# Hybrid attention and feed-forward kernel: when the feed-forward stage prepares what the window attention needs

## The chip, the cores and the metric

The kernel runs on one core of a Trainium2 chip, as one launch. The metric is the device time of the whole program in microseconds (us). Beside it stands the profile of one execution. The engines are called by their names: TensorE (PE), VectorE (DVE), ScalarE (ACT), GpSimd (POOL) and SyncE (SP).

## The reference

The input is 2 sequences of 2048 tokens with 256 features. Four blocks follow each other, each with a layer norm in front and a residual sum around it:

```python
x = x + retention_two_layers(_layernorm(x), ...)   # 2 x (retention, FFN of 1024)
x = x + ternary_ffn(_layernorm(x), w_up, w_down)
x = x + window_attention(_layernorm(x), Wq, Wk, Wv, Wo, q_gain, pair_mix)
x = x + ternary_ffn(_layernorm(x), w_up, w_down)
```

What matters for this change is the first `ternary_ffn` and the constants of the window attention:

```python
# ternary FFN: weights in {-1, 0, 1}, rows scaled by their root mean square
x_norm = x / (rms(x) + 1e-8)
h = gelu(x_norm @ w_up_ternary.T)          # 256 -> 1024
y = (h / (rms(h) + 1e-8)) @ w_down_ternary.T
# window attention: 16 query heads of 16, 4 key/value heads, a window of 64 keys
q = rotary(rms_norm(q)) * q_gain; scores = q @ k.T / sqrt(16), masked to the window
y = pair_mix applied to each pair of heads; out = y @ Wo.T
```

The kernel folds `pair_mix` into `Wo` ahead of time, and `1/sqrt(16)` into `q_gain`.

## The kernel before

The activations `X` stay in SBUF for the whole program, as 32 tiles of 128 tokens. The program is a row of stages: retention 0, feed-forward 0, retention 1, feed-forward 1, `ternary_ffn0`, the window attention, `ternary_ffn1`. Each stage is a block of five instruction streams, one for each engine, and between two stages all engines meet.

A feed-forward stage works on 8 blocks (`NB`) of 512 tokens. Each stream runs the same loop over a counter `g`, and the block worked on at step `g` is `b = g - 2`; steps 0 to 3 and 8 to 11 are written out, 4 to 7 are a hardware loop. Each step has 8 slots `m`, one for each 128 hidden features:

- TensorE multiplies the transposed input by the first weight (`up_product`, L719, into `hp`) and, two slots later, the hidden piece by the second weight (`down_product`, L730, into `yp`). Products are taken twice, with a high and a low half of the activations. In slots 3 and 5 it transposes the next block's normalised input `xn` (`transposes`, L746), both times through the same bank `tp`, so the second transposition waits until the first one's copy has been read.
- ScalarE applies the activation function twice, for the full value `h` and for the high half `h_hi` (L635, L636), squares six of the eight pieces (L642), and writes the high half of the transposed input (L649).
- VectorE computes the low half of each hidden piece (`hidden_low`, L472) and of the transposed input (`input_low`, L478), normalises the next block (`normalise`, L465), takes statistics of the one after that (L441, L449), and adds the scaled product to `X` (L501).
- GpSimd turns variances into scales, squares two pieces (L372) and adds the squares up (L380).

The first two blocks of `ternary_ffn0` have their statistics and scales from the stage before (`ready`, `KNOWN = 2`). GpSimd says so at the start of the stage by raising the semaphores `work_done` and `scale_done`. VectorE's `normalise(1)` in step `g = 2` waits for `scale_done`.

Beside its own work `ternary_ffn0` prepares the window attention (`window`). SyncE issues six loads into `staging` at the stage's start (`prefetch`, L68), the masks last, and all raise the semaphore `prefetched`; the wait for `16 * len(loads)` is a wait for all six. GpSimd clears five tiles (L295 to L301), and at the end of its step `g = 3` it prepares the gain (`window_gain`, L306 to L309). VectorE folds the pair mixing into the output weights (`mix_weights`, L546, L550, L555, L558, two instructions each) in slots 4 to 7 of step 2, and casts an identity twice (L579, L581) and the masks (L583) in slots 5 to 7 of step 3. Step 3 also has the low halves of the attention's weights (L85) in slots 0 and 1.

Each engine works its own stream in order. An instruction that waits holds everything behind it on that engine.

Of the kernel before, what the change touches and what calls it, by code (L numbers as in the profile page):

```python
# [35 lines left out]
NB = NT // TB  # L36
# [11 lines left out]
def apart(eng, waited):  # L48


    eng.sem_inc(waited, 1)  # L51
# [36 lines left out]
def at_third(idx):  # L88

    return isinstance(idx, int) and idx == 3  # L90
# [22 lines left out]
def ffn(nc, name, X, ident, lane, *, up, down, norm=None, hidden_bias=None, out_bias=None,  # L113
# [9 lines left out]
    ternary = norm is None  # L123
    R = 4
    with ExitStack() as c:  # L125
# [3 lines left out]
        def sem(n):  # L129
            return nc.alloc_semaphore(f"{name}_{n}")  # L130
# [50 lines left out]
        work_done = sem("work_done")  # L181
        scale_done = sem("scale_done")
# [30 lines left out]
        KNOWN = 2 if ready else 0  # L213
# [21 lines left out]
        def unmeasured(b):  # L235

            return live(b, MEASURED) and not (isinstance(b, int) and b < KNOWN)
# [45 lines left out]
        def _(pool):  # L283
# [4 lines left out]
            pool.wait_ge(powers_set, 4 if ternary else 3)  # L288
            if make_ternary:
                nc.gpsimd.memset(all_ones[:, :], 1.0).then_inc(ones_set, 1)  # L290
            if ready:
                pool.sem_inc(work_done, KNOWN * (5 if ternary else 1))
                pool.sem_inc(scale_done, KNOWN)
            if window is not None:
                nc.gpsimd.memset(window["minus_half"][:, :], -0.5)  # L295
                nc.gpsimd.memset(window["padded"][:, :, :, :, :], 0.0)
                nc.gpsimd.memset(window["kt"][:, :, :, :], 0.0)
                nc.gpsimd.memset(window["v_odd"][:, :, :, WD:SEG], 1.0)
                nc.gpsimd.memset(window["v_even"][:, :, :, :], 0.0).then_inc(v_cleared, 1)
                pool.wait_ge(v_cleared, 1)  # L300
                nc.gpsimd.memset(window["v_even"][:, :, :, WD:SEG], 1.0)  # L301

            def window_gain():

                gain = window["gain"]
                pool.wait_ge(prefetched, 16 * len(loads))  # L306
                nc.gpsimd.memset(gain[:, WH:WH + WKV], 1.0)
                apart(pool, pool_waited)
                nc.gpsimd.tensor_scalar(gain[:, 0:WH], gain[:, 0:WH], WD ** -0.5, None, ALU.mult)  # L309

            def work_before(b):

                return 5 * b if ternary else NB + 5 * (b - NB) if after_last(b) else b
# [89 lines left out]
            def body(i):  # L403
                for k in range(2):
                    g = 2 * i + k
                    b = g - 2
                    if not ternary:
                        if unmeasured(g):
                            scales(g, k)
                        if live(g - 1, NB):  # L410
                            add_constants(g - 1, i, k - 1)
                        continue
                    if live(b - 1, NB) and not final_block(b - 1):
                        add_squares(b - 1, 6)
                    if live(b, NB):
                        add_squares(b, 0)
                        pool_square(b, 3)
                        add_squares(b, 2)
                    if unmeasured(g):
                        if window is not None and last_block(g):  # L420
                            plain_scale(g, k)
                        else:
                            squared_scales(g, k)
                    if live(b - 1, NB):
                        rows_rms(b - 1)
                    if live(b, NB):
                        pool_square(b, 5)
                        add_squares(b, 4)
                    if window is not None and at_third(g):
                        window_gain()  # L430

            skewed(pool, body, N, first=2, last=2)

# [1 line left out]
        def _(dve):  # L435
# [103 lines left out]
            def mix_weights(step):  # L539

                wo, mix, out_hi, out_lo = window["wo"], window["mix"], window["out_hi"], window["out_lo"]
                for a in range(2):
                    if step == 0:
                        if a == 0:
                            dve.wait_ge(prefetched, 16 * len(loads))
                        nc.vector.tensor_scalar(mixed[:, 0, a, :], wo[:, 0, :], mix[:, 0, a:a + 1], None, ALU.mult  # L546
                                                ).then_inc(mix_first, 1)
                    if step == 1:
                        dve.wait_ge(mix_first, a + 1)
                        nc.vector.scalar_tensor_tensor(out=mixed[:, 1, a, :], in0=wo[:, 1, :],  # L550
                                                       scalar=mix[:, 1, a:a + 1], in1=mixed[:, 0, a, :],
                                                       op0=ALU.mult, op1=ALU.add).then_inc(mix_whole, 1)
                    if step == 2:
                        dve.wait_ge(mix_whole, a + 1)
                        nc.vector.tensor_copy(out_hi[:, a, :], mixed[:, 1, a, :]).then_inc(mix_high, 1)  # L555
                    if step == 3:
                        dve.wait_ge(mix_high, a + 1)
                        nc.vector.tensor_tensor(out_lo[:, a, :], mixed[:, 1, a, :], out_hi[:, a, :].bitcast(F32),  # L558
                                                ALU.subtract)

            def for_next_stage(g, m):

                if g == 2 and m == 4 and values is not None:
                    centre_values()
                if g == 3 and m < len(halves):
                    dve.wait_ge(hi_done, m + 1)
                    low_half(nc, halves[m])
                if g == 3 and m == 0 and make_ternary:
                    dve.wait_ge(w_summed, 4)
                    nc.vector.tensor_tensor(w_total[:, :], w_sums[:, :, 0], w_sums[:, :, 1], ALU.add  # L570
                                            ).then_inc(w_added, 1)
                if g == 3 and m == 4 and make_ternary:
                    weight_limits()
                if make_ternary and (g, m) in pieces_at:
                    ternary_piece(pieces_at[g, m])
                if g == 2 and window is not None and m >= 4:
                    mix_weights(m - 4)
                if g == 3 and window is not None and m == 5:
                    nc.vector.tensor_copy(window["ident_b"][:, :], ident[:, :])  # L579
                if g == 3 and window is not None and m == 6:  # L580
                    nc.vector.tensor_copy(window["ident_r"][:, :], ident[:, :])  # L581
                if g == 3 and window is not None and m == 7:
                    nc.vector.tensor_copy(window["masks"][:, :, :], window["win_masks"].rearrange("p v c u m -> p v (c u m)"))  # L583

            def body(i):
                for k in range(2):
# [1823 lines left out]
```

## Time and profile before

| what | us |
|---|---|
| three runs | 1547.82, 1549.32, 1544.11 |
| median | 1547.82 |
| the profiled execution, its own time | 1547.82 |
| its span (first to last instruction) | 1546.0 |
| TensorE busy, whole span | 1446.0 (94%) |
| VectorE busy | 1033.2 (67%) |
| ScalarE busy | 936.7 (61%) |
| GpSimd busy | 806.7 (52%) |
| mean granted clock of TensorE | 0.974 of full speed |

A time in a view is counted from the start of the span. The 1.8 us between the execution's time and its span lie around the first and the last instruction. "Busy" is the union of an engine's instructions; several matmuls overlap in it, so the distance between two starts says more of TensorE than the length of one.

### The profile page before, as it was taken

How to read it: one execution, taken by the hardware profiler on the slowest of the kernel's cores; microseconds unless marked ns; L12 is line 12 of the kernel's file. 1: busy time of each engine (PE TensorE's matmuls, PEld its weight loads, DVE VectorE, ACT ScalarE, POOL GpSimd, SP SyncE). 2: the span in 40 equal slices, each digit the busy share in tenths (PEclk: the TensorE clock that was granted, in tenths of full speed). 3: DMA queues.
4: the chain of work that ended last, by engine and by line, in shares of the span. 5: the costliest groups of instructions: out<-in, count | busy, mean ns of one | idle time of the engine just before them, and what ended most of it. 6: DMA issues, size and time to landing. Idle time of an engine off the chain costs nothing. (4 is left out here: it accounts for less than half of the span.)

```text
span 1546.0 us, 36706 instructions
## 1 busy us (share of the span) xinstructions
PE 1446.0 (94%) x13026; PEld 1201.1 (78%) x13058; DVE 1033.2 (67%) x2278; ACT 936.7 (61%) x1760; POOL 806.7 (52%) x844
## 2 busy tenths in 40 slices
PE   4999998899998999996999999995999999999998
PEld 3777876798996778885899888884777777767886
DVE  4777776455445887774655668773677777766774
ACT  5565563465553555553655557783677777767785
POOL 2566666211102666663431337764666666645774
PEclk9999998899999999997999999998999999999999
DMA  7000000100001000002100010000000000000011
GB/s 242 2 2 1 0 1 1 35 1 1 0 1 55 2 2 0 1 2 82 42 17 25 1 39 1 1 1 1 1 2 0 0 0 0 0 2 1 29 41 42
DMA packets 21090, 26.19 MB, mean 17 GB/s; under 512 B 1904, under 2 KB 19056, under 8 KB 20848
## 3 DMA queue, kind: packets, MB, share of 16 engines
q1 hardware_dynamic: 18432, 21.64, 4.2%
q10 hardware_dynamic: 2544, 3.04, 0.6%
q8 instruction: 70, 1.15, 0.3%
q14 instruction: 44, 0.36, 0.1%
HBM read 20.48 MB, written 4.19 MB: 16 GB/s over the span
## 5 line engine op out<-in xcount | busy, mean ns | idle before, releaser
L635 ACT ACTIVATE ffn_h<-ffn_hp,c_b 128x512 f32<-128x512 f32 x128 | 88.3, 690 | 171.4 <-PE ffn_hp L719 171.1
L472 DVE TENSOR_TENSOR ffn_h_lo<-ffn_h,ffn_h_hi 128x512 fp32r<-128x512 f32 x128 | 93.6, 731 | 144.0 <-ACT ffn_h_hi L636 143.8
L472 DVE TENSOR_TENSOR ternary_ffn_h_lo<-ternary_ffn_h,ternary_ffn_h_hi 128x512 fp32r<-128x512 f32 x128 | 108.3, 846 | 76.5 <-ACT ternary_ffn_h_hi L636 76.0
L730 PE MATMUL ffn_yp<-down_hi,ffn_h_hi 128*128 128x256 f32 x512 | 145.5, 284 | 0.0
L730 PE MATMUL ffn_yp<-down_hi,ffn_h_lo 128*128 128x256 f32 x512 | 142.8, 279 | 0.0
L730 PE MATMUL ffn_yp<-down_lo,ffn_h_hi 128*128 128x256 f32 x512 | 142.8, 279 | 0.0
L1029 POOL TENSOR_TENSOR ret_qk<-ret_qk,ret_qk_sin 128x512 f32<-128x512 f32 x64 | 82.7, 1292 | 102.8 <-DVE ret_qk_sin L1126 102.2
L730 PE MATMUL ternary_ffn_yp<-down_ternary,ternary_ffn_h_hi 128*128 128x256 f32 x512 | 128.4, 287 | 0.0
L1035 POOL TENSOR_TENSOR ret_rstd<-ret_sums,ret_minus_half 128x16 f32<-128x16 f32 x32 | 103.7, 3240 | 44.1 <-DVE ret_sums L1168 44.1
L730 PE MATMUL ternary_ffn_yp<-down_ternary,ternary_ffn_h_lo 128*128 128x256 f32 x512 | 123.4, 278 | 0.0
L1753 POOL TENSOR_TENSOR wa_rms<-wa_rms,win_minus_half 128x20 f32<-128x20 f32 x32 | 118.8, 3712 | 2.7
L380 POOL TENSOR_TENSOR ternary_ffn_h_sq<-ternary_ffn_h_sq 128x512 f32<-128x512 f32 x62 | 97.4, 1580 | 42.1 <-ACT ternary_ffn_h_sq L642 38.3
L1973 ACT ACTIVATE wa_probs_t<-wa_tp 128x512 f32<-128x512 f32 x128 | 76.4, 597 | 62.7 <-PE wa_tp L2143 62.2
L324 POOL TENSOR_SCALAR ffn_scale_work<-mean_var 128x4 f32<-128x4 f32 x13 | 3.6, 280 | 202.5 <-DVE mean_var L449 202.5
L635 ACT ACTIVATE ternary_ffn_h<-ternary_ffn_hp 128x512 f32<-128x512 f32 x128 | 76.5, 598 | 53.5 <-PE ternary_ffn_hp L719 47.2
L719 PE MATMUL ternary_ffn_hp<-xt_hi,up_ternary 128*128 128x512 f32 x256 | 103.6, 405 | 4.0 <-DVEq L618 4.0
L719 PE MATMUL ffn_hp<-xt_hi,up_hi 128*128 128x512 f32 x256 | 102.6, 401 | 4.4 <-DVEq L618 4.4
L719 PE MATMUL ternary_ffn_hp<-xt_lo,up_ternary 128*128 128x512 f32 x256 | 103.5, 404 | 0.0
L719 PE MATMUL ffn_hp<-xt_lo,up_hi 128*128 128x512 f32 x256 | 102.4, 400 | 0.0
L730 PEld LDWEIGHTS ternary_ffn_yp<-down_ternary,ternary_ffn_h_hi 128*128 128x128 f32 x512 | 96.4, 188 | 7.2 <-issue 3.8
L719 PE MATMUL ffn_hp<-xt_hi,up_lo 128*128 128x512 f32 x256 | 102.0, 398 | 0.0
L730 PEld LDWEIGHTS ffn_yp<-down_lo,ffn_h_hi 128*128 128x128 f32 x512 | 96.4, 188 | 4.3
(266 smaller groups left out, 4631.3 us busy)
## 6 DMA issues: line engine op xcount, KB each, us to landing
X<-in_x SPq DMA_DIRECT2D x8, 512.0 KB, 10.1
staging<-in_w SPq DMA_DIRECT2D x4, 1024.0 KB, 9.1
ffn_x_in<-in_x SPq DMA_DIRECT2D x8, 512.0 KB, 3.8
out<-X SPq DMA_DIRECT2D x7, 512.0 KB, 2.9
rotary<-in_rotary ACTq DMA_DIRECT2D x1, 1024.0 KB, 7.3
staging<-in_w_up SPq DMA_DIRECT2D x1, 1024.0 KB, 4.9
staging<-in_w_down SPq DMA_DIRECT2D x1, 1024.0 KB, 8.1
staging<-in_wqkv ACTq DMA_DIRECT2D x1, 768.0 KB, 6.1
```

The lines of the kernel that those rows point to most:

```text
L324: nc.gpsimd.tensor_scalar(work[:, 0, :], mv[:, k, :, 1], EPS, None, ALU.add).then_inc(work_done, 1)
L380: nc.gpsimd.tensor_tensor(h_sq[:, m, :], h_sq[:, m, :], h_sq[:, m + 1, :], ALU.add).then_inc(sq_added, 1)
L472: nc.vector.tensor_tensor(h_lo[:, m % R, :], h[:, m % R, :], h_hi[:, m % R, :].bitcast(F32), ALU.subtract).then_inc(h_ready, 1)
L635: nc.scalar.activation(h[:, m % R, :], hp[m % 2][:, :], fn, bias=bias)
L719: last = nc.tensor.matmul(hp[m % 2][:, :], w[:, j, m * P:(m + 1) * P], x[:, k, j, :], start=(n == 0), stop=(n == len(todo) - 1))
L730: last = nc.tensor.matmul(yp[k][t // 2][:, (t % 2) * D:(t % 2 + 1) * D], x[:, m % R, t * P:(t + 1) * P], w[:, m, :], start=(m == 0 and t % ...
L1029: nc.gpsimd.tensor_tensor(qk[:, r, :, :, :], qk[:, r, :, :, :], qk_sin[:, r, :, :, :], ALU.add).then_inc(qk_done, 1)
L1035: nc.gpsimd.tensor_tensor(rstd[:, :], sums[:, 1, :], minus_half[:, :], ALU.pow).then_inc(rstd_done, 1)
L1753: nc.gpsimd.tensor_tensor(rms[:, 1, :], rms[:, 0, :], minus_half[:, :], ALU.pow).then_inc(rms_work, 1)
L1973: nc.scalar.activation(pt[:, g, :, :].rearrange("p c n -> p (c n)"), tp[:, :], ACT.Copy).then_inc(pt_done, 1)
```

## The change

In `ternary_ffn0`, three pieces of preparation change their place; nothing is computed otherwise.

- GpSimd prepares the gain at the start of its stream instead of at the end of step 3, with the wait for the loads in front, and it raises `work_done` and `scale_done` after all of that instead of before.
- VectorE's four mixing steps move from step 2, slots 4 to 7, to step 3, slots 1, 3, 5 and 7.
- VectorE's three casts move from step 3, slots 5 to 7, to step 8 (`NB`): the masks in slot 6, both identities in slot 7.

```diff
             if make_ternary:
                 nc.gpsimd.memset(all_ones[:, :], 1.0).then_inc(ones_set, 1)
-            if ready:
-                pool.sem_inc(work_done, KNOWN * (5 if ternary else 1))
-                pool.sem_inc(scale_done, KNOWN)
             if window is not None:
+                gain = window["gain"]
                 nc.gpsimd.memset(window["minus_half"][:, :], -0.5)
...
                 pool.wait_ge(v_cleared, 1)
                 nc.gpsimd.memset(window["v_even"][:, :, :, WD:SEG], 1.0)
-
-            def window_gain():
-
-                gain = window["gain"]
                 pool.wait_ge(prefetched, 16 * len(loads))
                 nc.gpsimd.memset(gain[:, WH:WH + WKV], 1.0)
                 apart(pool, pool_waited)
                 nc.gpsimd.tensor_scalar(gain[:, 0:WH], gain[:, 0:WH], WD ** -0.5, None, ALU.mult)
+            if ready:
+                pool.sem_inc(work_done, KNOWN * (5 if ternary else 1))
+                pool.sem_inc(scale_done, KNOWN)
...
                         add_squares(b, 4)
-                    if window is not None and at_third(g):
-                        window_gain()
...
-                if g == 2 and window is not None and m >= 4:
-                    mix_weights(m - 4)
-                if g == 3 and window is not None and m == 5:
+                if g == 3 and window is not None and m in (1, 3, 5, 7):
+                    mix_weights(m // 2)
+                if g == NB and window is not None and m == 6:
+                    nc.vector.tensor_copy(window["masks"][:, :, :], window["win_masks"].rearrange("p v c u m -> p v (c u m)"))
+                if g == NB and window is not None and m == 7:
                     nc.vector.tensor_copy(window["ident_b"][:, :], ident[:, :])
-                if g == 3 and window is not None and m == 6:
                     nc.vector.tensor_copy(window["ident_r"][:, :], ident[:, :])
-                if g == 3 and window is not None and m == 7:
-                    nc.vector.tensor_copy(window["masks"][:, :, :], window["win_masks"].rearrange("p v c u m -> p v (c u m)"))
```

## Rows read from the trace of the kernel before

**Rows 1.** Waits of TensorE, 917 to 1056 us: us in total, times, longest.

```profile
PE ternary_ffn_tp L746 <- DVE xt_lo L478: 0.8, 2, 0.5
PE ternary_ffn_sqp L762 <- POOL ternary_ffn_h_sq L380: 0.4, 1, 0.4
```

**Rows 2.** Timeline of TensorE: start, length, in brackets the idle time before.

```profile
484.24 0.66 PE L1435 MATMUL ret_tr<-c_ident,ret_qk 128*128 128x128 f32 x4 [1.59 <-POOL ret_qk L1029]
...
913.48 0.50 PE L719 MATMUL ternary_ffn_hp<-xt_hi,up_ternary 128*128 128x512 f32 x1 [2.13 <-DVEq L618]
...
919.79 0.60 PE L746 MATMUL ternary_ffn_tp<-c_ident,xn 128*128 128x128 f32 x4
...
923.97 0.60 PE L746 MATMUL ternary_ffn_tp<-c_ident,xn 128*128 128x128 f32 x4
...
941.92 0.63 PE L746 MATMUL ternary_ffn_tp<-c_ident,xn 128*128 128x128 f32 x4 [0.55 <-DVE xt_lo L478]
...
1042.39 0.66 PE L746 MATMUL ternary_ffn_tp<-c_ident,xn 128*128 128x128 f32 x4
```

**Rows 3.** Stretches: us, busy of each engine, granted clock, DMA share, GB/s.

```profile
484.00:488.00 4.00, 3.76 (x50) 2.69 (x50) 2.63 (x7) 1.50 (x3) 0.18 (x1) 1.00 0.00 0
...
913.00:914.00 1.00, 0.52 (x2) 0.48 (x3) 0.00 (x0) 0.83 (x1) 0.67 (x6) 0.92 0.00 0
914.00:915.00 1.00, 1.00 (x3) 0.76 (x3) 0.00 (x0) 0.66 (x2) 1.00 (x2) 0.50 0.76 229
...
917.00:918.00 1.00, 1.00 (x5) 0.77 (x5) 1.00 (x5) 1.00 (x3) 0.00 (x0) 0.87 1.05 339
```

**Rows 4.** Timeline of SyncE's issues in `ternary_ffn0`, the last one.

```profile
915.45 0.68 SPq L68 DMA_DIRECT2D staging<-in_win_masks  x1
```

**Rows 5.** DMA issues, 900 to 960 us: size, us from issue to landing.

```profile
staging<-in_win_masks SPq DMA_DIRECT2D x1, 512.0 KB, 4.2
```

**Rows 6.** Timeline of GpSimd.

```profile
918.83 1.32 POOL L380 TENSOR_TENSOR ternary_ffn_h_sq<-ternary_ffn_h_sq 128x512 f32<-128x512 f32 x1 [2.08 <-ACT ternary_ffn_h_sq L642]
...
948.16 0.10 POOL L307 MEMSET staging<- 128x4 f32 x1
...
949.00 1.67 POOL L380 TENSOR_TENSOR ternary_ffn_h_sq<-ternary_ffn_h_sq 128x512 f32<-128x512 f32 x1
952.96 1.37 POOL L380 TENSOR_TENSOR ternary_ffn_h_sq<-ternary_ffn_h_sq 128x512 f32<-128x512 f32 x1 [2.29 <-ACT ternary_ffn_h_sq L642]
```

**Rows 7.** Timeline of VectorE.

```profile
917.02 1.38 DVE L465 TENSOR_SCALAR xn<-X,mean_var,scale 128x256 f32<-128x256 f32 x4
...
919.76 0.94 DVE L472 TENSOR_TENSOR ternary_ffn_h_lo<-ternary_ffn_h,ternary_ffn_h_hi 128x512 fp32r<-128x512 f32 x1
...
922.95 0.68 DVE L478 TENSOR_TENSOR xt_lo<-ternary_ffn_tp,xt_hi 128x512 fp32r<-128x512 f32 x1
...
924.65 0.61 DVE L546 TENSOR_SCALAR ternary_ffn_mixed<-staging 128x256 f32<-128x256 f32 x2
...
931.16 1.85 DVE L558 TENSOR_TENSOR win_out_lo<-ternary_ffn_mixed,win_out_hi 128x256 fp32r<-128x256 f32 x2
...
941.10 0.68 DVE L478 TENSOR_TENSOR xt_lo<-ternary_ffn_tp,xt_hi 128x512 fp32r<-128x512 f32 x1
...
947.00 1.34 DVE L581 CAST win_ident_r<-c_ident 128x128 fp32r<-128x128 f32 x1
...
948.83 0.68 DVE L583 CAST win_masks<-staging 128x1024 bf16<-128x1024 f32 x1
...
952.44 2.37 DVE L465 TENSOR_SCALAR xn<-X,mean_var,scale 128x256 f32 x4 [0.26 <-DVE scale L456]
...
1037.47 1.02 DVE L472 TENSOR_TENSOR ternary_ffn_h_lo<-ternary_ffn_h,ternary_ffn_h_hi 128x512 fp32r<-128x512 f32 x1 [0.16 <-ACT ternary_ffn_h_hi L636]
1038.42 1.37 DVE L465 TENSOR_SCALAR xn<-X,mean_var,scale 128x256 f32<-128x256 f32 x4
```

**Rows 8.** Timeline of ScalarE, the high half of block 1's first hidden piece.

```profile
931.46 0.59 ACT L636 ACTIVATE ternary_ffn_h_hi<-ternary_ffn_hp 128x512 fp32r<-128x512 f32 x1
```

## The prediction

> **What bounds the kernel now.** The change is confined to one stage, `ternary_ffn0`. I read it in four views.
>
> First, who TensorE waits for once the stage runs [rows 1]. Between 917 and 1056 us it waits 0.8 us for the low half of the transposed input (L478, VectorE) and 0.4 us for a sum of squares on GpSimd. That is all: TensorE sets the time of this stage, and work taken off another engine can return only those two waits. A stall put in front of TensorE, on the other hand, is paid in full, unless it fits into the lead that the other engine has.
>
> Second, TensorE's own order of time [rows 2]. The stage's first matmul starts at 913.48, after 2.13 us idle. The transposes of block 1 start at 919.79 for its first half and at 923.97 for its second. Those of block 2 start at 941.92, after 0.55 us idle: the larger of the waits for L478. These are the places where VectorE hands work to TensorE, so a late VectorE appears there.
>
> Third, the clock [rows 3]. After the 2.13 us idle at the stage's start the granted clock is 0.50, which is 1.2 GHz, and it is back at 1.00 (2.4 GHz) in the slice that starts at 917. From 0.92, 0.50 (three slices, one shown) and 0.87 the slow stretch is 0.16 + 3 + 0.26 = 3.4 us. After an idle time of 1.59 us elsewhere (484.24, in [rows 2]) the clock stayed at 1.00.
>
> Fourth, the loads and the three queues. SyncE issues the last of the six loads, the masks, at 915.45 [rows 4]. It lands 4.2 us after that [rows 5], at 919.65. GpSimd has finished its clearing and takes its first sum of squares at 918.83 [rows 6]. VectorE begins to normalise block 1 at 917.02 and needs 1.38 us, to 918.40 [rows 7].
>
> **The change part by part.**
>
> *GpSimd's signals (scale known, work done) move behind the gain's preparation.* That preparation waits for all six loads. The DVE instruction queued on the signal is the normalisation of block 1 at L465, and behind it on VectorE stand the low halves of the hidden activations from piece 1 on, the statistics of block 2, and the low halves of block 1's input. TensorE waits for each of them in turn. So the time at which the masks land, until now covered by nothing having to look at it before the first mixing step at 924.65 [rows 7], becomes the start of VectorE's work.
>
> - After 919.65 come the memset (0.10) and the multiplication. The next instruction began 949.00 - 948.16 = 0.84 us after the memset did [rows 6]; the memset's own 0.10 is the least. I bound the step by 0.1 and 0.84 and take 0.6, near the upper row but with VectorE idle beside it. The signal comes at 920.25.
> - The normalisation is late by 920.25 - 917.02 = 3.23 us and ends at 921.63. VectorE to TensorE costs some 0.14: L478 started at 941.10, ran 0.68, and the transposes started at 941.92 [rows 2, 7]. The first transposes come at 921.77 in place of 919.79: 1.98 us of stall.
> - L478 for block 1's first half ended at 922.95 + 0.68 = 923.63, and TensorE wanted it at 923.97: a lead of 0.34 only. VectorE's work up to there has almost no idle time in it (0.11 before 919.76, where it waited for ScalarE), so the delay carries through: 3.23 - 0.11 + 0.14 - 0.34 = 2.92 us late at the second transposes. That contains the first 1.98. Sum so far +2.92, with bounds of 2.4 and 3.2 from the step on GpSimd.
> - GpSimd itself starts its first sum at about 920.3 in place of 918.83. Its results are wanted at the end of the block, so I cost this at nothing; if that cover were gone it would be 1.5 us.
>
> *The mixing of the output weights moves from block 0 to block 1.* The last step ran at 931.16 for 1.85 us, to 933.01, and the next block's first low half had to wait behind it, although ScalarE's part was finished at 931.46 + 0.59 = 932.05 [rows 7, 8]. So VectorE enters the next block 0.96 us earlier. The first step (0.61) now stands in front of the input's low half of block 2, and the second one behind it. Net 0.35 us earlier, which comes off the 0.55 us idle at 941.92. Bounds: 0 (GpSimd's sums lengthen the steps) and 0.8, both waits of [rows 1] gone; on the other side one such collision, 0.99 us (below), could lengthen the wait by 0.7. I take -0.35. The third and fourth steps take the place of the casts at 947.00 (1.34) and 948.83 (0.68) and hit nothing.
>
> *The casts move to the block g = 8.* There the low half at 1037.47 waited 0.16 for ScalarE, the normalisation ended at 1038.42 + 1.37 = 1039.79, and its transposes came at 1042.39 [rows 2, 7]: a lead of 2.6 us, larger than the 1.34 + 0.68 + 0.3 moved there even if none fell into idle time. Cost nothing. Without that cover it would be 2.3 us.
>
> *The gain leaves GpSimd's queue at 948.16.* The 0.84 us that it frees end in a wait for ScalarE (2.29 idle before 952.96) [rows 6]. Nothing.
>
> Sum: 2.92 - 0.35 = +2.57 us, on the profiled execution's 1547.82 us, which is also the median of the runs: 1550.4 us.
>
> **The port between VectorE and GpSimd.** The four instructions of a normalisation took 1.38 us at 917.02 with GpSimd idle, and 2.37 at 952.44, where a sum of squares on GpSimd began at 952.96 [rows 6, 7]. After the change that first sum stands directly behind the signal that frees the normalisation. The Trainium skill (SBUF — State Buffer, "SBUF: two separate sides") says that the pair of ports is an exclusive lock, which whoever starts first keeps for its whole instruction. By that rule the sum would block the normalisation if it starts first; without it they would overlap at no cost.
>
> **The rivals.**
>
> 1. *The clock falls too.* The stall is 1.98 us; of two idle times seen, 1.59 left the clock at 1.00 and 2.13 was followed by 0.50 [rows 2, 3]. If it falls, 3.4 us at half speed cost 1.7. Part of the later 0.94 us of stall (2.92 - 1.98) then disappears behind a slow TensorE, so the net is 0.8 to 1.7. Time: 1551.2 to 1552.1, and 1553 together with the next one.
> 2. *GpSimd's sum gets in first.* The normalisation then takes 2.37 in place of 1.38, +0.99; the low half at 919.76, slowed to 0.94 by that same sum, returns 0.25. Time: 1551.1. By the skill's rule this is the case, unless VectorE wins the race.
> 3. *Nothing stalls, and the lighter block 0 counts.* TensorE wants the transposes only at 919.79; a signal by 918.3 costs nothing. That needs the masks to land 1.4 us earlier than the 4.2 of the trace. For it: the landing is one measurement, and all six loads share the time. Against: the issues themselves last until 915.45. What would be left is the gain of up to 0.8 us, and the time would be 1547.0. From a landing at 918.0 on this decides; it is the only case below the time of before.
> 4. *The moved mixing makes block 1 worse.* Its first step falls beside a sum of squares and adds 0.7 to the wait at 941.92 where I took 0.35 off: 1551.4.
>
> **How the numbers follow.** Forecast 0.36, clock 0.28, port alone 0.18, hidden 0.10, worse block 1 0.08. The forecast's own range is 1549.9 to 1551.0 by the bounds above. A measurement of this kernel can tell about 0.3% (4.6 us) from no change, seeing that three runs lie between 1544.11 and 1549.32. No case alone passes 1552.5; the clock together with the port comes near 1553, and with the spread of the medians about a quarter of the whole may show above it. So slower 0.23, same 0.72, faster 0.05. The range takes in the hidden case and the clock with the port: 1546.5 to 1554.0.
>
> **What would show it.** In the changed profile: (a) GpSimd's memset of the gain right behind the landing, near 919.7, with its idle time ended by the masks' load; (b) the normalisation of block 1 near 920.3, VectorE idle for 3 us before it; (c) the transposes near 921.8 and, for the second half, near 926.9; (d) the clock of the slices from 921 to 928; (e) a shorter wait at block 2's transposes; (f) no new wait of TensorE between 1035 and 1056. The prediction is wrong if TensorE's last matmul of the stage, relative to its first, moves by less than 1 or by more than 5 us, or if a stage other than this one changes by more than it does from run to run.

## The result, and the profile after

The changed kernel takes 1558.05 us (median of five runs, 1555.39 to 1559.16), the one before 1546.55 us: a ratio of 1.0069 with a 95% interval of 1.0052 to 1.0086, so 10.7 us slower by the ratio and 11.5 by the medians. I had forecast 2.6 us slower and a range that ended at 1554.0.

The two sets of times do not overlap: the slowest run before took 1549.32 us, the fastest changed one 1555.39.

The profiled execution has a span of 1555.8 us against 1546.0. The distance from the first matmul of `ternary_ffn0` to the first of the window attention, called the stage's length from here on, grew from 1061.41 - 913.48 = 147.93 us to 1070.38 - 911.15 = 159.23 us: 11.3 us. That is more than the 5 us at which the prediction called itself wrong. The first wait is at the place that was forecast, though three times as long; two more places, in blocks 2 and 7, were forecast to cost nothing. Who TensorE waits for in that stage (us in total, times, longest; between 914 and 1068 us, without a last line of 0.2 us for ScalarE), to be laid beside [rows 1]:

```profile
PE ternary_ffn_tp L740 <- DVE xn L460: 6.1, 1, 6.1
PE ternary_ffn_yp L724 <- DVE ternary_ffn_h_lo L467: 2.8, 2, 2.2
PE ternary_ffn_sqp L756 <- POOL ternary_ffn_h_sq L377: 0.4, 1, 0.4
PE ternary_ffn_tp L740 <- DVE xt_lo L473: 0.2, 1, 0.2
```

Two kinds of wait are new: 6.1 us for the normalisation of block 1, and 2.8 us in two pieces for the low half of a hidden piece. The changed timeline of TensorE at those places, and at the points that [rows 2] show:

```profile
911.15 0.50 PE L713 MATMUL ternary_ffn_hp<-xt_hi,up_ternary 128*128 128x512 f32 x1 [2.13 <-DVEq L612]
...
922.70 1.11 PE L740 MATMUL ternary_ffn_tp<-c_ident,xn 128*128 128x128 f32 x4 [6.11 <-DVE xn L460]
...
928.81 0.38 PE L740 MATMUL ternary_ffn_tp<-c_ident,xn 128*128 128x128 f32 x2
...
946.47 0.30 PE L740 MATMUL ternary_ffn_tp<-c_ident,xn 128*128 128x128 f32 x1 [0.25 <-DVE xt_lo L473]
...
959.45 0.38 PE L724 MATMUL ternary_ffn_yp<-down_ternary,ternary_ffn_h_hi 128*128 128x256 f32 x1 [2.19 <-DVE ternary_ffn_h_lo L467]
...
1048.64 0.38 PE L724 MATMUL ternary_ffn_yp<-down_ternary,ternary_ffn_h_hi 128*128 128x256 f32 x1 [0.62 <-DVE ternary_ffn_h_lo L467]
```

Counted from the stage's first matmul, the 11.3 us build up like this:

| place | before | changed | late by | forecast |
|---|---|---|---|---|
| transposes, block 1, first half | 6.31 | 11.55 | 5.24 | 1.98 |
| block 1, second half | 10.49 | 17.66 | 7.17 | 2.92 |
| block 2, second half | 28.44 | 35.32 | 6.88 | 2.57 |
| block 3, first half | 41.59 | 51.80 | 10.21 | 2.57 |
| first matmul of the next stage | 147.93 | 159.23 | 11.30 | 2.57 |

What stood behind the first wait, on GpSimd and then on VectorE (compare [rows 6, 7]); the line at 926.29 is the low half that the second transposes wait for:

```profile
918.03 0.10 POOL L301 MEMSET staging<- 128x4 f32 x1 [3.77 <-DMA staging<-in_win_masks]
918.48 0.27 POOL L303 TENSOR_SCALAR staging<-staging 128x16 f32<-128x16 f32 x1 [0.35 <-issue]
918.72 1.39 POOL L377 TENSOR_TENSOR ternary_ffn_h_sq<-ternary_ffn_h_sq 128x512 f32<-128x512 f32 x1
920.07 1.08 POOL L369 TENSOR_TENSOR ternary_ffn_h_sq<-ternary_ffn_h 128x512 f32<-128x512 f32 x1
921.24 1.26 POOL L377 TENSOR_TENSOR ternary_ffn_h_sq<-ternary_ffn_h_sq 128x512 f32<-128x512 f32 x1
```

```profile
918.58 4.07 DVE L460 TENSOR_SCALAR xn<-X,mean_var,scale 128x256 f32<-128x256 f32 x4 [4.38 <-POOLq L306]
...
926.29 0.68 DVE L473 TENSOR_TENSOR xt_lo<-ternary_ffn_tp,xt_hi 128x512 fp32r<-128x512 f32 x1
...
952.69 2.96 DVE L553 TENSOR_TENSOR win_out_lo<-ternary_ffn_mixed,win_out_hi 128x256 fp32r<-128x256 f32 x2
...
955.98 1.66 DVE L496 SCALAR_TENSOR_TENSOR X<-ternary_ffn_yp,ternary_ffn_inv_rms,X 128x256 f32 x4 [0.24 <-PE ternary_ffn_yp L724]
957.55 1.76 DVE L467 TENSOR_TENSOR ternary_ffn_h_lo<-ternary_ffn_h,ternary_ffn_h_hi 128x512 fp32r<-128x512 f32 x1
```

GpSimd's idle time ends with the masks' load, as forecast, and the signal comes 0.55 us after the memset. But then three operations were ready on GpSimd, not one, and the four instructions of the normalisation took 4.07 us instead of 1.38: the shortest of the four took 0.41 us, the longest 1.42. The clock fell as well (stretches as in [rows 3]):

```profile
920.00:923.00 3.00, 0.30 (x2) 0.30 (x3) 3.00 (x4) 0.00 (x0) 2.42 (x3) 0.50 0.00 0
923.00:926.00 3.00, 3.00 (x14) 2.90 (x13) 2.75 (x11) 0.60 (x1) 0.00 (x0) 0.50 0.00 0
926.00:927.00 1.00, 1.00 (x4) 0.77 (x4) 0.97 (x2) 0.00 (x0) 0.98 (x2) 0.59 0.02 8
...
961.00:964.00 3.00, 3.00 (x24) 1.93 (x23) 2.85 (x11) 1.09 (x2) 0.79 (x1) 0.50 0.03 5
```

The first fall begins while TensorE still stands idle; the second comes behind the 2.19 us wait.

At the stage's start it is the other way round. TensorE stands idle for 2.13 us there in both profiles, but the clock fell behind it only in the one before [rows 3]. Without that fall TensorE was ready for block 1's first transposes 5.44 us after its first matmul (11.55 less the wait of 6.11), where before it took them at 6.31. So 0.87 us of the 6.11 is a lead that it had gained, and the transposes are 5.24 us late.

### The profile page after: what moved, and what is told of

Same layout as the page of the kernel before. It is cut to its first block and busy times, and to the rows that moved or that the text cites. A ratio compares the mean times of both kernels' runs of the same rounds, so it can differ in the third digit from the quotient of the medians.

```text
span 1555.8 us, 36706 instructions
## 1 busy us (share of the span) xinstructions
PE 1447.1 (93%) x13026; PEld 1201.3 (77%) x13058; DVE 1036.1 (67%) x2278; ACT 936.5 (60%) x1760; POOL 804.5 (52%) x844
## 5 line engine op out<-in xcount | busy, mean ns | idle before, releaser
L467 DVE TENSOR_TENSOR ffn_h_lo<-ffn_h,ffn_h_hi 128x512 fp32r<-128x512 f32 x128 | 98.1, 768 | 142.3 <-ACT ffn_h_hi L630 142.2
L724 PEld LDWEIGHTS ternary_ffn_yp<-down_ternary,ternary_ffn_h_hi 128*128 128x128 f32 x512 | 97.4, 190 | 10.7 <-issue 6.2
```

What stands on the lines that cost most here:

```text
L467: nc.vector.tensor_tensor(h_lo[:, m % R, :], h[:, m % R, :], h_hi[:, m % R, :].bitcast(F32), ALU.subtract).then_inc(h_ready, 1)
L724: last = nc.tensor.matmul(yp[k][t // 2][:, (t % 2) * D:(t % 2 + 1) * D], x[:, m % R, t * P:(t + 1) * P], w[:, m, :], start=(m == 0 and t % ...
```

## The experiments

Each kernel is told as a short diff, with parts left out at `...`, against the kernel before or the changed one. The ratio is to runs of the kernel before that were taken with it. "Stage" is the stage's length in its profile. That is one execution, in which the landing of the masks (6.2 to 7.0 us after the stage's first matmul, where GpSimd waits for it) and the clock differ as well. In ten of the thirteen profiles the clock fell at the stage's start; in three it did not, after the same 2.13 or 2.14 us idle: the changed kernel, signals first and gain's own load. Signals first shows what that is worth: its first transposes come at 5.27 us instead of 6.31, and by block 2 nothing of it is left (28.40 against 28.44). The waits in the traces are the firmer evidence; differences of stages under about 1 us are not.

| kernel | ratio to before, 95% | stage, us |
|---|---|---|
| before | 1 | 147.93 |
| changed | 1.0069 (1.0052 to 1.0086) | 159.23 |
| signals first | 1.0022 (1.0011 to 1.0034) | 152.33 |
| GpSimd's part alone | 1.0051 (1.0037 to 1.0065) | 155.51 |
| VectorE's part alone | 1.0006 (0.9997 to 1.0015) | 148.88 |
| changed, sums held | 1.0037 (1.0024 to 1.0051) | 152.89 |
| casts alone | 1.0011 (1.0002 to 1.0020) | 148.27 |
| mixing alone | 1.0017 (1.0008 to 1.0026) | 151.26 |
| gain's own load | 1.0023 (1.0014 to 1.0031) | 152.20 |
| spacer | 1.0001 (0.9993 to 1.0010) | 149.60 |
| fourth step in slot 6 | 1.0011 (1.0002 to 1.0020) | 148.71 |
| GpSimd's part, sums held | 1.0024 (1.0014 to 1.0035) | 152.28 |
| late slots | 0.9996 (0.9987 to 1.0005) | 146.69 |

### Signals first

```diff
+            if ready:
+                pool.sem_inc(work_done, KNOWN * (5 if ternary else 1))
+                pool.sem_inc(scale_done, KNOWN)
             if window is not None:
                 gain = window["gain"]
...
                 nc.gpsimd.tensor_scalar(gain[:, 0:WH], gain[:, 0:WH], WD ** -0.5, None, ALU.mult)
-            if ready:
-                pool.sem_inc(work_done, KNOWN * (5 if ternary else 1))
-                pool.sem_inc(scale_done, KNOWN)
```

> The changed kernel with the two signals raised at the very start again, ahead of the clearing and the gain; everything else as changed. A stage length is the distance from the first matmul of the ternary stage to the first of the window attention: 147.9 us before, 159.2 changed. Theory A (the signals behind the wait for the loads cost most of it, and the two moves on VectorE cost the rest through waits at 959.45 and 1048.64 us): the 6.1 us wait of the first transposes is gone, the stage is 150.5 to 152 us long, the program 3 to 4 us above before. Rival B (VectorE's moves cost only because the stall has already made it late): stage 147.5 to 148.5, the program equal to before. Rival C (the gain's preparation at the start costs by itself, since GpSimd's first sum waits behind it): a wait of TensorE for a sum of squares in block 0.

Measured: stage 152.33, just above theory A's band; ratio 1.0022, 3.4 us above before, inside it. The 6.1 us wait is gone, so putting the two signals back is worth 6.9 us of the stage. Its waits of TensorE:

```profile
PE ternary_ffn_yp L724 <- DVE ternary_ffn_h_lo L467: 3.1, 3, 2.2
...
PE ternary_ffn_tp L740 <- DVE xt_lo L473: 0.8, 2, 0.4
PE ternary_ffn_sqp L756 <- POOL ternary_ffn_h_sq L377: 0.4, 1, 0.4
```

The waits for the hidden low half stand without any stall in front of them, so they do not come from the late signal. Rival C is out: there is no wait for a sum of squares in block 0, and the one of 0.4 us stands in block 7, as before.

### GpSimd's part alone, VectorE's part alone

The changed kernel with VectorE's lines of before, and the kernel before with VectorE's lines of the change.

> The kernel before with GpSimd's part of the change alone (gain at the start, signals behind it); mixing and casts where they were. Theory A: the first transposes wait some 6 us, the clock falls behind them, stage 154.5 to 156 us, program 7 to 8 us above before. Rival B: the whole 11 us, stage near 159, because the stall is what makes VectorE late everywhere. Forecast's own size (2.9 us of stall): stage near 151.

> The kernel before with both moves on VectorE (mixing to block 1, casts to block 6), GpSimd's stream as before. Theory A: waits of TensorE for a low half of a hidden piece behind the fourth mixing step and behind the casts, 2 to 3.5 us together, with up to 1.7 more where the clock falls; stage 150.5 to 152, like the first kernel of this set. Rival B: no new wait, stage 147.5 to 148.5.

GpSimd's part alone: stage 155.51 (+7.58), inside theory A's band, and the only new wait is the one for the normalisation (5.2 us); the normalisation again takes 4.07 us. VectorE's part alone: stage 148.88 (+0.95), where theory A had 150.5 to 152 and rival B 147.5 to 148.5: both missed, and the run time cannot be told from before. The two parts sum to 8.5 us of stage, the whole is 11.3. The run times alone would not show that difference (0.51% and 0.06% against 0.69%, each known to 0.1 or 0.2%); the traces do. The 2.2 us wait behind the fourth mixing step does not exist when GpSimd's stream is as before, although all of VectorE's moves are made:

```profile
PE ternary_ffn_yp L729 <- DVE ternary_ffn_h_lo L472: 0.6, 1, 0.6
PE ternary_ffn_sqp L761 <- POOL ternary_ffn_h_sq L380: 0.4, 1, 0.4
PE ternary_ffn_tp L745 <- DVE xt_lo L478: 0.2, 1, 0.2
```

With these moves of VectorE, the wait needs something from GpSimd's part as well. Theory A had it as VectorE's alone, and fell there. The place is narrow: from block 2's second transposes to block 3's first the kernel before takes 13.15 us, VectorE's part alone 13.50, signals first 16.46 and the changed kernel 16.48. The fourth mixing step, and GpSimd beside it, in VectorE's part alone:

```profile
946.19 1.85 DVE L558 TENSOR_TENSOR win_out_lo<-ternary_ffn_mixed,win_out_hi 128x256 fp32r<-128x256 f32 x2
```

```profile
945.60 1.82 POOL L380 TENSOR_TENSOR ternary_ffn_h_sq<-ternary_ffn_h_sq 128x512 f32<-128x512 f32 x1
947.36 0.10 POOL L307 MEMSET staging<- 128x4 f32 x1
...
947.80 1.40 POOL L380 TENSOR_TENSOR ternary_ffn_h_sq<-ternary_ffn_h_sq 128x512 f32<-128x512 f32 x1
```

The step takes 1.85 us with the gain between the two sums, and 2.96 in the changed kernel. The spacer below tests whether that is the reason.

### Changed, sums held

```diff
                 pool.sem_inc(scale_done, KNOWN)
+            if window is not None:
+                pool.wait_ge(xn_done, 2)
```

> The changed kernel in which GpSimd, after raising the signals, waits until VectorE has finished normalising block 1 before it starts its first sum of squares. It only delays GpSimd. Theory A (three operations on GpSimd standing ready behind the signal each stop one instruction of the normalisation, 4.07 us in place of 1.38): the normalisation takes 1.4 us again, the first transposes wait 3.4 us instead of 6.1, stage 155 to 157, the program 2.5 to 4 us below the changed kernel although one engine does its work later. Rival D (the normalisation is slow for another reason, such as the landing loads): it stays near 4 us and the stage at 159 or above.

A kernel that only makes GpSimd wait is faster than the changed one: ratio 1.0037 against 1.0069, stage 152.89. Its VectorE and GpSimd:

```profile
919.40 1.38 DVE L462 TENSOR_SCALAR xn<-X,mean_var,scale 128x256 f32<-128x256 f32 x4 [3.01 <-POOLq L306]
```

```profile
918.85 0.10 POOL L301 MEMSET staging<- 128x4 f32 x1 [3.10 <-DMA staging<-in_win_masks]
919.30 0.27 POOL L303 TENSOR_SCALAR staging<-staging 128x16 f32<-128x16 f32 x1 [0.35 <-issue]
920.87 1.66 POOL L379 TENSOR_TENSOR ternary_ffn_h_sq<-ternary_ffn_h_sq 128x512 f32<-128x512 f32 x1 [1.29 <-DVE xn L462]
```

The normalisation is back to 1.38 us although it still waits for the signal, so the 2.7 us were the three operations. The wait was 1.71 us, and the clock did not fall behind it: 1.00 in both stretches from 920 to 926. The gain was larger than expected (6.3 us of the stage, expected about 2 to 4), and not all of it is the sums'. The first transposes come 3.36 us earlier: 2.69 from the normalisation and 0.68 from the masks, which landed earlier in this execution (VectorE starts 6.75 us after the first matmul instead of 7.43). At block 2 the lead is 3.66 us. The remaining 2.7 us come behind it: the wait behind the fourth mixing step shrank to 1.09 us, after which the clock stayed up too. Why it shrank was not tried; the step took 2.95 us here as well.

### GpSimd's part alone, sums held

The same added wait in the kernel with GpSimd's part alone, to have the ports' share without the mixing.

> GpSimd's part of the change alone (stage 155.5, program 0.51% above before), with GpSimd waiting for the normalisation before its first sum. Theory A: the normalisation takes 1.4 us instead of 4.07, the first transposes come near 8.2 us after the first matmul instead of 11.7; the clock either stays or falls for one stretch instead of two; stage 150.5 to 152.5, and the share of the ports in this part is 3 to 5 us. Rival: the freed time is given back because GpSimd's scale for block 2 comes late, seen as a wait in block 1; stage above 153.

Stage 152.28 instead of 155.51; normalisation 1.38 us. The first transposes come at 8.99 us, not near 8.2, since the masks landed late in this execution (7.0 us after the first matmul, as in GpSimd's part alone). TensorE's wait was 2.53 us, and here the clock fell behind it, for 3.4 us instead of 6.8. The rival finds nothing: the scale of block 2 comes in time. Of GpSimd's part, 3.2 us are the ports with what the clock adds, and 4.35 us the late signal with what the clock adds.

### Gain's own load

The changed kernel, with a semaphore of its own for the gain's load (SyncE raises `gain_loaded` for the fourth load and `prefetched` for the other five).

```diff
-                pool.wait_ge(prefetched, 16 * len(loads))
+                pool.wait_ge(gain_loaded, 16)
...
-                            dve.wait_ge(prefetched, 16 * len(loads))
+                            dve.wait_ge(prefetched, 16 * LOADS)
```

> The changed kernel in which the gain's load, the fourth of six, raises a semaphore of its own, and GpSimd waits for that one alone. Theory A (the stall is the landing of the last load plus the sums that stand ready by then): the signal comes some 4.7 us after the first matmul instead of 7.4, GpSimd's first sum is hardly ready by then, the normalisation takes 1.4 to 2.4 us, the first transposes wait 0 to 1.5 us, the clock does not fall there, stage 151.5 to 154 (waits of blocks 2 and 7 remain). Rival (order behind the gain's own work costs, not the landing): stage near 159.

Stage 152.20, in the band; ratio 1.0023.

```profile
917.50 0.10 POOL L306 MEMSET staging<- 128x4 f32 x1 [1.21 <-DMA staging<-in_q_gain]
917.96 0.27 POOL L308 TENSOR_SCALAR staging<-staging 128x16 f32<-128x16 f32 x1 [0.35 <-issue]
918.19 1.40 POOL L382 TENSOR_TENSOR ternary_ffn_h_sq<-ternary_ffn_h_sq 128x512 f32<-128x512 f32 x1
920.49 1.41 POOL L374 TENSOR_TENSOR ternary_ffn_h_sq<-ternary_ffn_h 128x512 f32<-128x512 f32 x1 [0.89 <-ACT ternary_ffn_h_hi L635]
```

```profile
918.06 2.34 DVE L465 TENSOR_SCALAR xn<-X,mean_var,scale 128x256 f32<-128x256 f32 x4 [1.83 <-POOLq L311]
```

The signal comes 4.9 us after the first matmul instead of 7.4. Only one sum is ready by then, and the normalisation takes 2.34 us. With the two kernels above this makes a series: none, one and three operations ready on GpSimd, and 1.38, 2.34 and 4.07 us. The first transposes waited 1.85 us, longer than the 0 to 1.5 expected, and the clock fell behind that wait, against my expectation.

### Casts alone, mixing alone

```diff
 # casts alone: mixing in block 0 as before, casts out of block 1, and
+                if g == NB and window is not None and m == 6:
+                    nc.vector.tensor_copy(window["masks"][:, :, :], ...)
+                if g == NB and window is not None and m == 7:
+                    nc.vector.tensor_copy(window["ident_b"][:, :], ident[:, :])
+                    nc.vector.tensor_copy(window["ident_r"][:, :], ident[:, :])
 # mixing alone: casts in block 1 as before, and
-                if g == 2 and window is not None and m >= 4:
-                    mix_weights(m - 4)
+                if g == 3 and window is not None and m in (1, 3, 5, 7):
+                    mix_weights(m // 2)
```

> The kernel before with the three casts alone moved to block 6. Theory A (the casts put 2 to 3.3 us in front of the residual and the low half of block 7, whose lead is smaller than that): one wait of TensorE of 0.6 to 0.9 us for a low half near 127 us after the stage's first matmul, stage 148.5 to 149, program within 0.1% of before. Rival (that wait comes from VectorE being late from further ahead): no such wait, stage 147.9 or less.

> The kernel before with the four mixing steps alone moved to block 1, gain and casts as before. Theory A (the mixing is harmless there as long as GpSimd prepares the gain between its two sums): no wait for a hidden low half behind the fourth step, the wait for the input's low half of block 2 shrinks from 0.55 to about 0.25 us, stage 147.4 to 148.3. The casts stand in slots 5 to 7 as well here, so VectorE carries 2.3 us more in that block than in the changed kernel: if that is too much, a wait of up to 2 us shows between 40 and 47 us.

The casts alone bring the 0.62 us wait of TensorE at block 7, inside theory A's 0.6 to 0.9. The stage is 148.27, below its band, and ahead of block 7 the trace shows why: in block 3 the second transposes come at 45.77 us, where before they waited 0.23 for VectorE and came at 46.30. Leaving block 1 returns some 0.56 us, and the new place costs 0.90. VectorE at block 7:

```profile
1030.31 0.89 DVE L472 TENSOR_TENSOR ternary_ffn_h_lo<-ternary_ffn_h,ternary_ffn_h_hi 128x512 fp32r<-128x512 f32 x1 [0.56 <-ACT ternary_ffn_h_hi L635]
1031.12 1.31 DVE L581 CAST win_ident_b<-c_ident 128x128 bf16<-128x128 f32 x1
1032.35 1.33 DVE L582 CAST win_ident_r<-c_ident 128x128 fp32r<-128x128 f32 x1
...
1035.98 2.35 DVE L465 TENSOR_SCALAR xn<-X,mean_var,scale 128x256 f32<-128x256 f32 x4
```

Each identity took 1.3 us beside two sums on GpSimd (1030.73, 2.87 us), where in the mixing alone it took 0.21 and 0.22 with no sum or square beside it. The mixing alone missed theory A's band (147.4 to 148.3): it is 3.3 us longer than before (151.26). The 2.19 us wait and the clock's fall appear, although the gain stands on GpSimd where it stood. This kernel differs from VectorE's part alone, which has no such wait, in the casts alone, which stay in block 1 here; theory A had named that case. VectorE:

```profile
947.06 1.86 DVE L558 TENSOR_TENSOR win_out_lo<-ternary_ffn_mixed,win_out_hi 128x256 fp32r<-128x256 f32 x2
948.84 1.78 DVE L583 CAST win_masks<-staging 128x1024 bf16<-128x1024 f32 x1
950.55 0.17 DVE L490 RECIPROCAL ternary_ffn_inv_rms<-ternary_ffn_rms 128x4 f32<-128x4 f32 x1
950.95 1.66 DVE L501 SCALAR_TENSOR_TENSOR X<-ternary_ffn_yp,ternary_ffn_inv_rms,X 128x256 f32 x4 [0.24 <-DVE ternary_ffn_inv_rms L490]
952.53 1.16 DVE L472 TENSOR_TENSOR ternary_ffn_h_lo<-ternary_ffn_h,ternary_ffn_h_hi 128x512 fp32r<-128x512 f32 x1
```

The fourth step is short here, but the masks' cast behind it takes 1.78 us instead of 0.68. So the wait of block 2 can be had without touching GpSimd. What the cases with it have in common is more time between the start of the fourth step and the reciprocal in front of the residual sum: 3.5 us here (947.06 to 950.55) and 2.9 in signals first and in the changed kernel, against 1.8 in VectorE's part alone. The size of the wait does not follow from it alone.

### Spacer

Signals first, with the gain's two operations repeated at the end of GpSimd's step 3, the multiplication by 1.

```diff
                         add_squares(b, 4)
+                    if window is not None and at_third(g):
+                        nc.gpsimd.memset(gain[:, WH:WH + WKV], 1.0)
+                        apart(pool, pool_waited)
+                        nc.gpsimd.tensor_scalar(gain[:, 0:WH], gain[:, 0:WH], 1.0, None, ALU.mult)
```

> The first kernel of the first set (signals at the very start, gain at the start, VectorE's moves as changed), with the gain's memset and a multiplication by 1 repeated at the end of GpSimd's step 3, where the kernel before had the gain. It only adds work to GpSimd. Theory A (the 0.84 us there kept two sums of squares apart, and without it the fourth mixing step and the next low half lose the ports twice): the fourth step takes 1.9 us instead of 2.96, the 2.2 us wait in block 2 and the clock's fall behind it are gone, stage 148.5 to 149.5 instead of 152.3, program 2.5 to 4 us faster for added work. Rival (the wait comes from the mixing steps' own length or from GpSimd's delayed start): stage stays near 152.3.

Added work on GpSimd makes the kernel faster: ratio 1.0001 against 1.0022, stage 149.60 against 152.33, with 13.76 us instead of 16.46 from block 2's second transposes to block 3's first. GpSimd and VectorE with the spacer:

```profile
946.89 1.61 POOL L377 TENSOR_TENSOR ternary_ffn_h_sq<-ternary_ffn_h_sq 128x512 f32<-128x512 f32 x1
948.46 0.09 POOL L427 MEMSET staging<- 128x4 f32 x1
948.62 0.31 POOL L429 TENSOR_SCALAR staging<-staging 128x16 f32<-128x16 f32 x1
948.89 1.40 POOL L377 TENSOR_TENSOR ternary_ffn_h_sq<-ternary_ffn_h_sq 128x512 f32<-128x512 f32 x1
```

```profile
947.29 1.84 DVE L557 TENSOR_TENSOR win_out_lo<-ternary_ffn_mixed,win_out_hi 128x256 fp32r<-128x256 f32 x2
```

And without it, in the kernel with the signals first:

```profile
947.54 3.06 POOL L377 TENSOR_TENSOR ternary_ffn_h_sq<-ternary_ffn_h_sq 128x512 f32<-128x512 f32 x2
```

```profile
947.94 2.96 DVE L553 TENSOR_TENSOR win_out_lo<-ternary_ffn_mixed,win_out_hi 128x256 fp32r<-128x256 f32 x2
```

Without the spacer each of the step's two instructions took about 1.5 us, as long as one sum. With the gain between the sums, the second instruction gets through.

### Fourth step in slot 6

Signals first, the fourth mixing step one slot earlier.

```diff
-                if g == 3 and window is not None and m in (1, 3, 5, 7):
-                    mix_weights(m // 2)
+                if g == 3 and window is not None and m in (1, 3, 5, 6):
+                    mix_weights((m + 1) // 2 if m == 6 else m // 2)
```

> The first kernel of the first set (signals first; it has a 2.2 us wait behind the fourth mixing step in slot 7 and a stage of 152.3 us) with that fourth step one slot earlier, in slot 6. Theory A (the place counts: between slot 7 and the next low half stands the residual sum, and VectorE has no lead there, while slot 6 has over 1 us of idle time): the wait at 41 us after the first matmul and the clock's fall are gone or under 0.7 us, stage 148.8 to 150. Rival (the volume of work in block 1 counts, wherever it stands): the wait stays near 2 us, stage near 152.

Stage 148.71 instead of 152.33, a little below the band: the 2.19 us wait is gone, with the same work in the same block and the gain still at the start. Place, not volume. The run times point the same way (1.0011 against 1.0022) but do not prove it, since their intervals overlap.

### Late slots

GpSimd's stream as before; VectorE's work where the profile before shows idle time behind the slot. The old places (steps 2 and 3) are empty.

```diff
+                if g == NB and window is not None and m == 4:
+                    mix_weights(0)
+                if g == NB and window is not None and m == 6:
+                    nc.vector.tensor_copy(window["masks"][:, :, :], ...)
+                if g == NB + 1 and window is not None and m in (4, 5, 6):
+                    mix_weights(m - 3)
+                if g == NB + 2 and window is not None and m == 2:
+                    nc.vector.tensor_copy(window["ident_b"][:, :], ident[:, :])
+                    nc.vector.tensor_copy(window["ident_r"][:, :], ident[:, :])
```

> An attempt at a faster version than both: GpSimd's stream as before; the mixing steps in step 8 slot 4 and step 9 slots 4 to 6, the masks in step 8 slot 6, both identities in step 10 slot 2, where VectorE has 0.8 to 1.7 us of idle time per slot. Theory A (only places with idle time behind them are free): no wait for VectorE in blocks 1 to 3 except up to 0.3 us, none behind the moved work, stage 147.0 to 147.6, program 0 to 1 us below before, which the runs can hardly tell from no change. Rival (anything moved costs): stage above 148.

Stage 146.69, 1.2 us below before and below the 147.0 expected, and after the first matmul the trace shows no wait of TensorE in the whole stage, not even those of [rows 1], which sum to 1.2. In run time the ratio is 0.9996 (0.9987 to 1.0005): as forecast, too little to be told from no change.

## Why the prediction was wrong

**What bounds the stage: right, but not for the first two blocks.** The kernel that moves VectorE's work to really idle places gains the waits of [rows 1] and no more. Up to block 2's second transposes VectorE sets the time as well: the microsecond that signals first had won by its clock was lost again there, around two new waits for VectorE of 0.36 and 0.27 us.

**The signal behind the loads: right in mechanism, sized a little low.** "The step on GpSimd" was taken as 0.6 us; from the memset to VectorE's start it was 0.55. The masks landed 6.8 us after the stage's first matmul instead of 6.2 (and between 6.2 and 7.0 in the other kernels in which GpSimd waits for them), so the normalisation began 7.43 us after it against 3.54, a delay of 3.89 where I had 3.23. I had taken one landing as a constant. The rival with an early landing did not happen. Its condition was also misworked: for a signal by 918.3 the masks would have had to land 1.95 us earlier by my own 0.6 us for the step, not 1.4.

**The port: the step that failed.** I named the mechanism, priced it at one sum (+0.99), gave it 0.18 as a rival and left it out of the sum. Three operations were ready by then: two sums and a square. VectorE's four instructions took 0.41 us (the shortest) to 1.42 (the longest), 4.07 together in place of 1.38, and ended 0.15 us behind the third operation. The first transposes are late by the signal's 3.89 and these 2.69 us, less the 1.34 that lay between the normalisation's end and the transposes before and no longer does: 5.24 where I had 1.98. The mistake lies in "GpSimd itself starts its first sum at about 920.3": I looked at which operation was next in the queue, not at how many had become ready while the queue stood still. The series 1.38, 2.34 and 4.07 us for none, one and three, and the kernel with the sums held, show it; in GpSimd's part alone, holding the sums gives back 3.2 us of the stage. The rule of the Trainium skill (SBUF — State Buffer, "SBUF: two separate sides"), that whichever of the two engines starts first keeps the shared pair of ports for its whole instruction and the other is blocked, agrees with these rows. What the change costs by it depends on counting instructions on both sides.

**The clock: a rival with 0.28, and it happened.** The changed profile shows 0.50 in the stretches from 920 to 926. The fall began inside the 6.11 us wait and lasted some 6.8 us, twice the 3.4 of my price; about 4 of them lie behind the wait, where TensorE had work. From the first to the second transposes the lateness rises from 5.24 to 7.17 us. VectorE had finished the low half for them at 926.97, and they started 1.84 us later, at 928.81: that part I put down to the clock, an estimate near the 1.7 priced. A rise alone would not show it, since with the sums held it was 1.6 us with the clock at 1.00, through a wait of 1.20 us for VectorE. The clock fell a second time behind the 2.19 us wait.

**"The third and fourth steps take the place of the casts and hit nothing": failed.** I compared durations measured in another place. In slot 7 the fourth step stands directly before the residual sum and the next low half, and there it met two sums in a row (2.96 us instead of 1.85). From block 2's second to block 3's first transposes the lateness rises by 3.3 us: 2.19 us of wait, the rest not taken apart; the clock's fall lies in it.

**"The gain leaves GpSimd's queue. Nothing": failed.** I followed the 0.84 us on GpSimd and found that nobody waited for its results. But the two operations of the gain stood between two sums, and in that gap VectorE got through. The spacer puts it back and returns 2.7 us of the stage. This is the term that belongs to neither part alone: 7.6 + 0.95 against 11.3 us. It holds for the casts in block 6; with the casts in block 1 the same wait came with the gain in place.

**"The casts: cost nothing": failed, by 0.9 us at the new place.** 2.6 us of lead was counted to the transposes, the wrong consumer. The hidden low half of block 7 is wanted earlier, and there TensorE waited 0.62 us, since both identities took 1.3 us each. That leaving block 1 would return 0.56 us, as the casts alone show, was not in the sum either.

**The lighter block 0: the number fits, the reason is not shown.** Block 2's second transposes made up 0.29 us (7.17 to 6.88), forecast 0.35, and VectorE's part alone made up 0.31. But the mixing alone made up only 0.12, and GpSimd's part alone, with the mixing still in block 0, made up 0.71. A late TensorE makes up time there by itself, so the 0.29 may be luck.

Open: the clock. A wait of 1.71 us was not followed by a fall, one of 1.85 us was, and the 2.13 us idle at the stage's start was followed by one in ten profiles but not in three, the changed one among them, where the stretches from 911 to 920 show 1.00. What decides between the two was not tried. How much of the interaction comes from the moment at which each collision falls was not tried either.

## What to carry to other kernels

When a stream that waits moves in front of a signal, count what becomes ready behind the wait: it starts all at once when the signal goes out, beside the very work that the signal frees, and each short instruction of that work can be held for a whole one of the other engine's. A cheap operation that nobody waits for may be holding two others apart, so taking it away can cost more than it returns. Work moved into another engine's gaps belongs behind a slot with measured idle time and not just before the consumer with the smallest lead.

## What was not expected of the hardware

- VectorE's short instructions and GpSimd's long ones took turns: four instructions, 1.38 us together when alone, took 4.07 us beside three operations of 1.1 to 1.4 us, and 2.34 us beside one.
- The same cast of a 128x128 identity took 0.22 us with no sum or square on GpSimd beside it, and 1.3 us beside sums.
- A wait of 1.85 us was followed by the clock's fall to 1.2 GHz in one kernel, while 2.13 us idle passed without one in another.
- The last of six loads landed 4.2 us after its issue in the profile before, 4.8 us in the changed one and up to 5.0 in others; a wait for it moved by as much.
